# Context attention on one Trainium2 core: the fp16 exponential becomes a copy, taken one step later

## What is computed

```python
q = _ln((x @ Wq + bq).reshape(b, s1, H, HD), qn_w, qn_b)
k = _ln(kv[..., :HD], kn_w, kn_b)          # kv = y_main @ [Wk, Wv] + [bk, bv]
v = kv[..., HD:]
s = jnp.einsum('bhqd,bhkd->bhqk', q, k) * SCALE
p = jax.nn.softmax(s, axis=-1)
ctx = jnp.einsum('bhqk,bhkd->bhqd', p, v)
```

## Time and profile before

| | |
|---|---|
| Time, median of 3 runs | 3063.67 us (3058.69 to 3066.0) |
| Time of the profiled execution | 3058.08 us |
| Span of the profiled execution | 3056.3 us |
| PE busy | 2793.6 us (91%) |
| DVE busy | 2558.9 us (84%) |
| ACT busy | 2268.2 us (74%) |
| POOL busy | 1612.8 us (53%) |
| Exponentials to fp32 (L420), 128 x 1024 and short, `ps_t` to `e` | 428, 409.7 us |
| Exponentials to fp16 (L422), the same | 428, 410.8 us |
| Low parts (L335) | 428, 854.5 us |

### The profile page before, as it was taken

The page is one execution under the profiler, slowest core; times in us unless marked ns, Lnnn a source line. Parts: engine busy times, 40 slices in busy tenths (PEclk is TensorE's granted clock), DMA queues, the critical chain, the costliest instruction groups (busy, mean ns, idle before and its releaser), DMA issues. The chain is left out here.

```text
span 3056.3 us, 103347 instructions
## 1 busy us (share of the span) xinstructions
PE 2793.6 (91%) x42025; PEld 1761.7 (58%) x42025; DVE 2558.9 (84%) x4146; ACT 2268.2 (74%) x4155; POOL 1612.8 (53%) x2006
## 2 busy tenths in 40 slices
PE   7789999999999778789996779999999999968889
PEld 3346666666666556577774435666666666645646
DVE  6599999999999656768885779999999999957752
ACT  5479999999999754446664448999999999963431
POOL 1257777777777543212223326777777777752200
PEclk9899999999999889899998989999999999979989
DMA  4354654554554244348885345545545555430020
GB/s 127 86 96 84 98 91 87 97 88 88 96 89 83 56 160 153 133 165 302 302 305 152 102 88 87 98 87 89 96 89 90 94 89 96 75 91 1 1 75 28
DMA packets 542754, 329.52 MB, mean 108 GB/s; under 512 B 459382, under 2 KB 504566, under 8 KB 536523
## 3 DMA queue, kind: packets, MB, share of 16 engines
q1 hardware_dynamic: 534314, 295.63, 43.7%
q0 software_dynamic: 7680, 25.17, 2.7%
q10 hardware_dynamic: 288, 2.10, 0.2%
HBM read 181.86 MB, written 36.09 MB: 71 GB/s over the span
## 5 line engine op out<-in xcount | busy, mean ns | idle before, releaser
L335 POOL TENSOR_TENSOR a_elo<-a_e 128x1024 f16<-128x1024 f32 x428 | 854.5, 1997 | 272.4 <-ACT a_e L422 272.4
L592 PE MATMUL a_ps_k<-l_wk,a_yh 128*64 128x512 f16 (+1 forms) x3200 | 580.2, 386 | 32.2 <-POOL a_yl L317 22.0
L592 PE MATMUL a_ps_v<-l_wv,a_yh 128*64 128x512 f16 (+1 forms) x3200 | 577.5, 384 | 17.4 <-DVE a_v L482 16.8
L493 DVE TENSOR_REDUCE a_mx<-a_ps_m 128x2 f32<-128x1024 f32 x384 | 466.7, 1215 | 13.3 <-PE a_ps_m L618 12.0
L420 ACT ACTIVATE a_e<-a_ps_t 128x1024 f32<-128x1024 f32 x428 | 409.7, 957 | 33.6 <-PE a_ps_t L652 27.3
L422 ACT ACTIVATE a_e<-a_ps_t 128x1024 f16<-128x1024 f32 x428 | 410.8, 960 | 0.0
L652 PE MATMUL a_ps_t<-a_qb,a_kk 64*128 64x128 f16 (+1 forms) x9672 | 351.1, 219 | 8.1 <-ACT a_e L422 7.8
L652 PEld LDWEIGHTS a_ps_t<-a_qb,a_kk 64*128 64x128 f16 (+1 forms) x9672 | 281.5, 96 | 120.1 <-issue 88.6
L592 PE MATMUL a_ps_k<-l_wk,a_yl 128*64 128x512 f16 (+1 forms) x1600 | 322.6, 383 | 0.0
L592 PE MATMUL a_ps_v<-l_wv,a_yl 128*64 128x512 f16 (+1 forms) x1600 | 320.6, 380 | 0.0
L592 PEld LDWEIGHTS a_ps_k<-l_wk,a_yh 128*64 128x64 f16 (+1 forms) x3200 | 191.3, 110 | 221.1 <-issue 49.4
(11 more groups left out here) (415 smaller groups left out, 5316.0 us busy)
## 6 DMA issues: line engine op xcount, KB each, us to landing
l_land<-in_ctx SPq DMA_DIRECT2D x96, 384.0 KB, 3.8
l_ob<-in_m_w SPq DMA_DIRECT2D x32, 1024.0 KB, 7.9
f_w<-in_m_w SPq DMA_DIRECT2D x32, 512.0 KB, 4.9
eo_dram<-f_e_eo SPq DMA_DIRECT2D x32, 512.0 KB, 4.6
l_land<-in_ctx SPq DMA_DIRECT2D x32, 433.0 KB, 4.4
a_kk<-a_khl SPq DMA_TRANSPOSE x416, 3.1
qs_dram<-p_q SPq DMA_DIRECT2D x32, 128.0 KB, 2.4
dca_dram<-p_od SPq DMA_DIRECT2D x16, 256.0 KB, 2.4
```

Of the source, the lines that this page charges most:

```text
L335: pool.tensor_tensor(rest[0:r, :, 0:w], full[0:r, :, 0:w], high[0:r, :, 0:w], ALU.subtract)\
L493: dve.tensor_reduce(mx[:, g, :, c], ps_m[:, :, :], AX.X, ALU.max).then_inc(mx_done, 1)
L592: m = pe.matmul(out[half:half + h, :], part[:, n % 2, c, o + half:o + half + h], w[:, wpart, c, :], start=(c == 0 and a == 0), stop=(c == ...
```

## The change

The step `e` keeps its first instruction alone, which now signals a new semaphore `x_done`. A new step `ec` makes the fp16 value: it copies `e32` (SBUF) to `e16` and signals `e_done`. In ScalarE's order `ec` stands one step behind its `e`. TensorE's next scores wait for `x_done` in place of `e_done`. `lo` and `pv` wait for `e_done` as before.

```diff
--- before.py
+++ after.py
@@ -53,10 +53,11 @@
     PE: k2- pv6-- m7-- s8-- v0- k3- pv7-- s9-- m8-- pv8-- v1- k4- s10-- m9-- v2- pv9-- m10-- s11-- k5- m11--
     PE: v3- s12-- m12-- pv10-- v4- tb-- k6- s13-- v5- k7- pv11-- v6- k8- s0- pv12-- pv13-- k9- v7- s1- m0-
     PE: k10- pv0- s2- m1- v8- k11- m2- s3- pv1-
-    ACT: e5-- rp10-- vh11-- sq0- kh10-- e6-- rp11-- r6-- vh12-- yh1- kh11-- e7-- rp12-- sq1- e8-- kh12-- sq2-
-    ACT: vh0- r0- sq3- e9-- rp0- vh1- kh0- e10-- vh2- rp1- r1- sq4- e11-- yh2- vh3- kh1- sq5- e12-- rp2- vh4-
-    ACT: r2- kh2- qh-- sq6- rp3- vh5- yh3- kh3- e13-- rp4- sq7- vh6- kh4- r3- sq8- rp5- e0- kh5- vh7- rp6- e1-
-    ACT: sq9- kh6- e2- vh8- sq10- rp7- yh0 r4- kh7- e3- rp8- vh9- sq11- kh8- e4- rp9- vh10- sq12- r5- kh9-
+    ACT: e5-- rp10-- ec5-- vh11-- sq0- kh10-- e6-- rp11-- ec6-- r6-- vh12-- yh1- kh11-- e7-- rp12-- ec7-- sq1-
+    ACT: e8-- kh12-- ec8-- sq2- vh0- r0- sq3- e9-- rp0- ec9-- vh1- kh0- e10-- vh2- ec10-- rp1- r1- sq4- e11--
+    ACT: yh2- ec11-- vh3- kh1- sq5- e12-- rp2- ec12-- vh4- r2- kh2- qh-- sq6- rp3- vh5- yh3- kh3- e13-- rp4-
+    ACT: ec13-- sq7- vh6- kh4- r3- sq8- rp5- e0- kh5- ec0- vh7- rp6- e1- sq9- ec1- kh6- e2- vh8- ec2- sq10- rp7-
+    ACT: yh0 r4- kh7- e3- rp8- ec3- vh9- sq11- kh8- e4- rp9- ec4- vh10- sq12- r5- kh9-
     DVE: kl10-- m5-- hat11-- kc1- rd0- m6-- kl11-- vl12-- kc2- hat12-- rd1- o0-- m7-- kc3- vl0- m8-- kl12--
     DVE: rd2- hat0- vl1- rd3- m9-- kl0- kc4- m10-- vl2- hat1- m11-- kc5- vl3- m12-- kl1- t-- rd4- rd5- hat2-
     DVE: qs-- vl4- kc6- kl2- ql-- hat3- vl5- kc7- kl3- rd6- hat4- rd7- kc8- kl4- vl6- hat5- o1-- kc9- kl5-
@@ -148,7 +149,7 @@
         vh_done, vl_done = sem("vh_done"), sem("vl_done")
         qm_done, sm_done, mx_done, mxx_done = sem("qm_done"), sem("sm_done"), sem("mx_done"), sem("mxx_done")
         tb_done, q1_done, qh_done, ql_done = sem("tb_done"), sem("q1_done"), sem("qh_done"), sem("ql_done")
-        s_done, e_done, lo_done, pv_done = sem("s_done"), sem("e_done"), sem("lo_done"), sem("pv_done")
+        s_done, x_done, e_done, lo_done, pv_done = sem("s_done"), sem("x_done"), sem("e_done"), sem("lo_done"), sem("pv_done")
         rl_done, os_done, o_done = sem("rl_done"), sem("os_done"), sem("o_done")
         low_done = sem("low_done")
 
@@ -351,6 +352,7 @@
             def _(act):
                 act.preload_act_table_set("natural_log_exp_and_others")
                 act.sem_inc(e_done, 1)
+                act.sem_inc(x_done, 1)
                 act.wait_ge(const_ok, 2)
 
                 def y_high(at, c):
@@ -417,9 +419,16 @@
                         wait_low(act, n - 2)
                     elif j >= 4:
                         wait_low(act, n - 4)
-                    act.activation(full[0:r, :, 0:w], src[0:r, :, 0:w], ACT.Exp)
+                    act.activation(full[0:r, :, 0:w], src[0:r, :, 0:w], ACT.Exp).then_inc(x_done, 1)
+
+                def exponent_high(at, j):
+
+                    n = at.b * UNITS + j
+                    full, high, _ = e_set(at, j)
+                    r, w = extent(j)
+                    act.wait_ge(x_done, n + 2)
                     wait_values(act, at, j)
-                    act.activation(high[0:r, :, 0:w], src[0:r, :, 0:w], ACT.Exp).then_inc(e_done, 1)
+                    act.activation(high[0:r, :, 0:w], full[0:r, :, 0:w], ACT.Copy).then_inc(e_done, 1)
 
                 def step(kind, i, at):
                     if kind == "yh":
@@ -438,8 +447,10 @@
                         q_high(at)
                     elif kind == "e":
                         exponent(at, i)
-
-                batches("ACT", ("e",), step)
+                    elif kind == "ec":
+                        exponent_high(at, i)
+
+                batches("ACT", ("e", "ec"), step)
 
             @block.vector
             def _(dve):
@@ -638,9 +649,9 @@
                         wait_turned(pe, at.b * KT + KT)
                     dst = scores_in(at, j)
                     if at.b < B - 1 or j == 0:
-                        pe.wait_ge(e_done, n + 1)
+                        pe.wait_ge(x_done, n + 1)
                     elif j >= 2:
-                        pe.wait_ge(e_done, n)
+                        pe.wait_ge(x_done, n)
                     for i in tiles_of(j):
                         k = slice(i * P, i * P + rows(i))
                         for gl in range(2):
```

## The result

The changed kernel takes 3168.8 us (median of 4 runs, 3161.3 to 3170.7), the kernel before 3062.5 in the same comparison: the ratio is 1.0343, with an interval of 1.0321 to 1.0365. It is slower by 3.4%, 106 us. The profiled execution has a span of 3168.9 us, 112.6 more than before.

The account below looks back on a forecast made before the run. PE sets the pace, DVE one per cent behind; 1.5 + 0.5 + 1.2 less 0.1 is 3.1 us per period, times 28 is 87, plus 4 is 91: 3149, on the median 3155 us; range 3078 to 3225.

Parts of the forecast that it names:

- Place 1: Units 5 to 8: ACT's waits for DVE's input make lo late; PE is 1.5 us late per period at pv8.
- e7: ACT's exponential step of unit 7; the step behind it, asked for 0.90 us earlier, would find its input not ready.
- Place 2: Unit 10: ACT's wait for PE's projection makes lo late; PE is 0.5 us late per period at pv10.
- Place 3: Unit 2: ACT's wait for PE's projection makes lo late; PE is 1.2 us late per period at pv2.
- Other units: Elsewhere in the period, added waits on ACT of 0.1 to 0.9 us overlap the three places or end in idle time.
- The number of periods: 14 periods per layer, so whatever is gained or lost in one period counts 28 times.
- e0: ACT's exponential step of unit 0, which marks a period's start; e0 to e0 forecast near 60.1 us in place of 57.0.
- The last batch: There the copy directly follows and waits for its exponential; 2 us per layer, 4 us together.
- B, absorbed: Rival: waits on ACT vanish in its free time; about 0.9 us per period remains, 3093 us; chance 0.20.
- C, the full waits: Rival: DVE and PE follow every wait for inputs, about 6 us per period, 3240 us; chance 0.10.
- D, the earlier bank decides: Rival: not slower, as PE starts scores sooner; at most 20 us gained, 3044, at least no change; chance 0.15.
- the earlier bank: The scores' banks come free 0.9 us earlier for PE; counted as nothing, at most 0.1 us per period.

Follow-up runs that it names:

- moved_exp: The change with the deferred copy replaced by the old exponential from PSUM, and the next scores waiting for it; 3212.4 us, ratio 1.0522 to the kernel before.
- other_units: The kernel before with only units 0, 1, 3, 4, 9, 11, 12 and 13 deferred (exponential, next step, then copy); 3078.5 us, ratio 1.0083.
- copy_adjacent: The change with each of the 14 copies right behind its exponential, banks still freed at the first; 3082.3 us, ratio 1.0083 to the kernel before.
- pair_wait: The kernel before with one wait added: the second exponential, still from PSUM, waits until the first has ended; 3089.2 us, ratio 1.0116.
- only_e5_e8: The kernel before with only units 5 to 8 deferred (exponential, next step, then copy); 3104.0 us, ratio 1.0154.
- ready_only: The kernel before with only units 1, 11 and 12 deferred, where input lies ready and pv has room; 3057.8 us, ratio 1.0003.

## Why the prediction was right

The forecast was 3155 us, +91 on the profiled execution; +112.6 came (3168.8 in the median of the runs). The mechanism held, step by step:

- *ACT's own time.* Forecast: the copy costs 10 to 40 ns more, 0.94 us from start to start in place of 0.90. Measured: 26 ns longer, and 0.95 us from start to start (650.58 to 651.53); moved_exp says that it hardly matters.
- *Place 1.* Forecast 1.5 us at pv8, measured 1.76 by pv8 in the change and 1.68 alone. Mis-sized was the lateness carried in from e5: I took 0.4 and the runs show 0.6 to 0.7 (ScalarE 0.73 late at kh11 and e7). And rp10's wait ends with the root from GpSimd and not with kl9: the move of the earlier step was limited by two inputs, of which I had checked one. The waits list has both, 11.2 and 11.0 us in 400.
- *Place 2.* Forecast 0.5, measured 0.6, and 0.5 alone.
- *Place 3.* Forecast 1.2, measured 1.2, and 1.20 alone.
- *Other units.* Forecast: overlapping or hidden. pv0's 0.2 us was neither; it made 6 us in 28 periods. The 0.48 at v2 (other_units) does overlap.
- *The number of periods.* I counted 14 per layer. The fifteenth, from e0 of batch 14 (1045.29) to e0 of batch 15 (1098.33), is 53.0 us where it was 49.8, another 6.5 us in two layers.
- *The last batch.* Forecast 2 us per layer. In the first layer 33.3 us pass from its e0 to the load of ScalarE's next table (1098.33 to 1131.67), 33.1 before (1044.97 to 1078.06). The pairs did get longer, 2.02 us from pair to pair in place of 1.82, but ScalarE's idle time ahead of later scores fell from 3.5 to 1.4 us and took that up. In the second layer it is 35.2 us (2809.33 to 2844.49) against 32.3 (2700.71 to 2732.99), 2.9 more, at a granted clock of 0.75 against 0.82 over that stretch; in the first layer it was 0.86 in both kernels. How much of the 2.9 is the clock's, no run separates. That the mean, 1.6, lies near my 2 is in part luck.
- *The overlap.* What the Trainium skill (ScalarE: Activation LUTs, "What ACT_TABLE_LOAD costs") says of the overlap of back-to-back ACTIVATEs, about 93 ns, lies near the trace: an exponential of 1.02 us and what follows it stand 0.90 us apart, an overlap of 0.12, and a copy of 1.04 us and its successor 0.95 apart (650.58 and 651.53), 0.09. With the wait in copy_adjacent the two stand 1.04 us apart, and no overlap is left. pair_wait shows what that costs in the whole program: 1.2%.

The sum by what the first layer measured, doubled: 28 x 3.76 = 105, the fifteenth periods 6.5, the last batches 0.5, together 112. With both layers read, it divides a little otherwise: from e0 of batch 0 to e0 of batch 15 the first layer is 55.9 us longer and the second 54.6 (1907.43 to 2809.33 against 1853.40 to 2700.71), and the last batches are 0.3 and 2.9 longer. That is 113.6 together; the rest of the program is 1.0 shorter, which gives the 112.6 measured.

The rivals: B, absorbed (3093), falls with only_e5_e8 alone, whose four units lose 46 us where B has 29 for all. C, the full waits (3240), falls, since the waits for inputs overlap, as other_units shows: eight deferrals lose 0.6 us per period. D, the earlier bank decides, falls with ready_only and copy_adjacent.

One statement of the forecast was incomplete: that the earlier bank counts for nothing. It gives nothing where it was tried in the old order (three units), but the new order would cost 167 us and not 106 without it. I never wrote down what the new order asks of the scores, since the change brought debt and payment together.

## What to carry to other kernels

Where three in-order queues are all nearly full, the price of a moved instruction is set less by its own duration than by two rooms: how long the input of the step that is pulled ahead has lain ready, and how long the consumer of the step that is put back waits behind its producer already. Read both from the timeline for each place, and sum only the places where PE, which sets the pace, has none; here three places made four fifths of the losses (97 of 119 us, taken one by one). A second instruction that recomputes from the same input can be better than a copy of the first one's result: right behind the first it has no wait between them, and that wait alone cost 1.2% here.

## What the runs showed of the hardware

- A ScalarE instruction that waits for the end of its predecessor starts some 0.03 us after it (599.53 + 1.01 = 600.54, next start 600.57), where GpSimd starts 0.08 and PE 0.14 us after the end of what they wait for (lo8 and pv8 in the timeline after). I had taken 0.08 for ScalarE too.
- The copy of 128x1024 from SBUF takes 1046 ns and the exponential of the same size from PSUM 1015 to 1020, a difference of 3%.
